# Narrow attentions: dividing and projecting each batch inside the steps, with the head sums passed through DRAM

## Time and profile before

| | us |
|---|---|
| median of 3 runs | 1738.42 (1737.92 to 1742.84) |
| profiled execution, its own time | 1742.06 |
| its span, first to last instruction | 1740.3 |
| PE busy | 1470.2 (84%) |
| DVE busy | 1009.0 (58%) |
| ACT busy | 797.1 (46%) |
| POOL busy | 455.9 (26%) |

### The profile page before, as it was taken

One profiled execution on the slowest core, in us unless ns is written; L12 is line 12 of the kernel. 1 busy time (PEld: TensorE's weight loads), 2 busy tenths in 40 slices (PEclk: granted clock), 3 DMA queues, 4 the chain that ended last, 5 costly groups with the idle time before them and its releaser, 6 DMA issues. The chain is left out here.

```text
span 1740.3 us, 30717 instructions
## 1 busy us (share of the span) xinstructions
PE 1470.2 (84%) x10727; PEld 738.2 (42%) x10747; DVE 1009.0 (58%) x1970; ACT 797.1 (46%) x1479; POOL 455.9 (26%) x658
## 2 busy tenths in 40 slices
PE   7998999999749999679876898889836888888887
PEld 5777634444424445246533442222404333433354
DVE  5665598884352222465547578997274574567335
ACT  3554537677213333215330136777434365346535
POOL 6121300000144443320126230000003354245311
PEclk9999999999969999699887898999957899989878
DMA  2000443110200000001000163121001520342000
GB/s 95 1 0 0 146 161 93 42 49 8 117 0 0 1 0 0 0 7 49 5 6 0 57 198 110 50 54 29 15 0 44 169 70 21 98 157 66 11 16 24
DMA packets 82246, 85.67 MB, mean 49 GB/s; under 512 B 7228, under 2 KB 67900, under 8 KB 81756
## 3 DMA queue, kind: packets, MB, share of 16 engines
q1 hardware_dynamic: 82152, 84.45, 15.2%
HBM read 51.33 MB, written 32.51 MB: 48 GB/s over the span
## 5 line engine op out<-in xcount | busy, mean ns | idle before, releaser
L1282 ACT ACTIVATE arena<-ps 128x1024 f32<-128x1024 f32 x256 | 261.9, 1023 | 112.1 <-PE ps L1191 111.2
L1176 PE MATMUL ps<-k_stack,q_stack 49*128 49x512 bf16 x512 | 192.3, 387 | 15.3 <-DVE small L1306 13.2
L1191 PE MATMUL ps<-q_stack,k_stack 51*128 51x256 bf16 x1024 | 191.3, 275 | 0.5 <-ACT arena L1282 0.4
L1303 DVE CUSTOM_DVE_ANT_0 small<-ps,mask_b 128x512 bf16<-128x512 f32 x256 | 168.0, 689 | 33.7 <-PE ps L1176 32.3
L1306 DVE TENSOR_REDUCE small<-ps 128x1 f32<-128x512 f32 x256 | 162.1, 685 | 22.6 <-PE ps L1176 21.6
L1492 DVE TENSOR_REDUCE small<-ps 128x6 f32<-128x768 f32 x128 | 122.6, 958 | 77.8 <-PE ps L1374 75.7
L1203 PE MATMUL ps<-arena,v_pad 128*32 128x256 f32 x2048 | 163.7, 394 | 1.1 <-ACT arena L1282 1.1
L1468 ACT ACTIVATE arena<-ps 128x384 f32<-128x384 f32 x256 | 117.8, 488 | 76.5 <-PE ps L1393 75.8
L1076 POOL TENSOR_SCALAR_AFFINE_SELECT arena<-arena 128x256 f32<-128x256 f32 x256 | 101.9, 406 | 84.2 <-ACT arena L1468 84.0
L2543 DVE TENSOR_TENSOR arena<-ps,arena 128x512 f32<-128x512 f32 x64 | 44.3, 692 | 120.8 <-PE ps L2509 120.8
L2558 POOL TENSOR_TENSOR arena<-arena 128x512 f32<-128x512 f32 x64 | 80.9, 1264 | 108.9 <-DVE arena L2543 107.1
(11 more groups left out here) (353 smaller groups left out, 3036.2 us busy)
## 6 DMA issues: line engine op xcount, KB each, us to landing
q_stack<-q_scratch SPq DMA_DIRECT2D x128, 96.0 KB
k_stack<-k_scratch SPq DMA_DIRECT2D x64, 192.0 KB
k_scratch<-arena SPq DMA_DIRECT2D x8, 768.0 KB, 3.6
k_stack<-k_scratch SPq DMA_DIRECT2D x64, 96.0 KB
q_scratch<-arena SPq DMA_DIRECT2D x4, 1152.0 KB, 5.4
arena<-in_ctxT SPq DMA_DIRECT2D x8, 512.0 KB, 6.6
k_scratch<-arena SPq DMA_DIRECT2D x8, 512.0 KB, 4.7
k_scratch<-arena SPq DMA_DIRECT2D x16, 256.0 KB, 4.5
```

What stands on the lines that cost most here:

```text
L1176: pe.matmul(ps[:, t, :], c.q_stack[par][64 * e:64 * e + ROW_MAX, pr, t * P:(t + 1) * P], c.k_stack[par][64 * e:64 * e + ROW_MAX, pr, :], s ...
L1191: mm = pe.matmul(ps[:, bank, (ch % 2) * S:(ch % 2 + 1) * S], c.k_stack[prv][64 * e:64 * e + ROWS, pr, ch * P:(ch + 1) * P], c.q_stack[prv] ...
L1282: act.activation(buf.probs[i % 8], ps[:, bank:bank + 2, :].rearrange("p a n -> p (a n)"), ACT.Exp, scale=scale).then_inc(g["probs"].sem, 1)
L1303: dve.tensor_tensor_reduce(buf.junk[t], ps[:, t, :], c.mask_b[:, M_X + t * SC:M_X + (t + 1) * SC], 1.0, FLOOR, op0=ALU.add, op1=ALU.max, a ...
```

## The change

The stage `combine` is removed. A new class `Outputs` does its work for batches 0 to 4 inside the steps, four steps behind the scores, and for batches 5 to 7 behind the last step, in the same block.

For each batch b except the last, SP stores the 128 rows of summed groups (512 KB) to a DRAM scratch in step b+2, and loads the numerators back as 128 rows of 256 columns (128 KB), and the denominators as 128 rows of 32 columns (16 KB); DVE inverts these in step b+3 (`invert`, with the guard where there is one); SP stores the inverses (16 KB) and loads them spread over the 8 channels of a head (128 KB). In step b+4 the quotient is taken (POOL in the wide attentions, DVE in the short ones), multiplied by the gate on POOL where there is one, and projected by PE at position 7 into bank 7; in the wide attentions ACT copies the result with its bias and POOL adds it to x, in the short ones DVE adds it. Before PE writes head sum group 1 into bank 7 again it waits for that copy, or that addition. Behind the last step batch 5 is finished, batch 6 is inverted as 128 rows of 256 columns, and batch 7's sums are collected, inverted and spread by PE without DRAM.

`attend_steps` writes steps 0 to 3 and 8 out and loops over 4 to 7. The gate is made in `project`, in front of its `keep_clock`. The constants are loaded in two parts. In the feed-forward of the last layer some semaphores have other names.

```diff
@@ project @@
+            if gated:
+                for t in TS:
+                    if t < 2:
+                        pe.wait_ge(g["ln_scaled"].sem, g["ln_scaled"].at(4))
+                    else:
+                        pe.wait_ge(g["gate_out"].sem, g["gate_out"].at(t - 1))
+                    pe.matmul(ps[:, 2 + t % 2, :], w[:, W_G:W_G + P], norm.tile(c.xn, t), start=True, stop=True)\
+                      .then_inc(g["gate_in"].sem, 1)
...
             keep_clock(c, pe, PARTS_WAIT, bank=bank_of(kind, n))
...
+            if gated:
+                for t in TS:
+                    act.wait_ge(g["gate_in"].sem, g["gate_in"].at(t + 1))
+                    act.activation(norm.tile(c.xn, t), ps[:, 2 + t % 2, :], ACT.Sigmoid, bias=w[:, W_BG:W_BG + 1])\
+                       .then_inc(g["gate_out"].sem, 1)
@@ Outputs @@
+    def store_sums(self, buf, sp, b):
+        for i in range(2):
+            sp.wait_ge(g[f"summed_out{i}"].sem, g[f"summed_out{i}"].at(2 * b + 2))
+        sp.dma_start(c.sum_scratch[b, :, :, :].rearrange("r j m -> j r m"), ...).then_inc(g["sums_stored"].sem, 16)
+    def load_sums(self, sp, b, last=False):
+        sp.wait_ge(g["sums_stored"].sem, g["sums_stored"].at(16 * (b + 1)))
+        if b > 1:
+            done, n = self.quotient(b - 2)
+            sp.wait_ge(done.sem, done.at(n + 1))
+        sp.dma_start(self.num[b % 2], c.sum_scratch[b, 0:DH, :, :].rearrange("d j (k n) -> (d j k) n", n=S)).then_inc(sem, 16)
+        if last:
+            self.spread(sp, self.rec[b % 2], c.sum_scratch[b, DH, :, :].rearrange("j (k n) -> (j k) n", n=S), sem)
+        else:
+            sp.dma_start(self.den[b % 2], ...).then_inc(sem, 16)
+    def store_inverse(self, sp, b):
+        sp.wait_ge(g["inverted"].sem, g["inverted"].at(b + 1))
+        sp.dma_start(c.inv_scratch[b, :, :].rearrange("q (a n) -> (q a) n", a=P // H), self.den[b % 2]).then_inc(g["inv_stored"].sem, 16)
+    def spread_inverse(self, sp, b):
+        sp.wait_ge(g["inv_stored"].sem, g["inv_stored"].at(16 * (b + 1)))
+        self.spread(sp, self.rec[b % 2], c.inv_scratch[b, :, :], g[f"inv_spread{b % 2}"].sem)
+    def finish_pe(self, buf, pe, scored):
+        self.project(pe, 1, B - 3, 0)
+        self.project(pe, 0, B - 2, 1)
+        for k in range(GROUPS):
+            den = pe.matmul(c.ps[0:H, 3, 0:S], ..., buf.summed[:, B - 1, k, :], ...)
+            num = pe.matmul(c.ps[:, 4, 0:S], ..., buf.summed[:, B - 1, k, :], ...)
+        keep_clock(c, pe, 6, bank=2)
+        pe.wait_ge(g["inverted"].sem, g["inverted"].at(B))
+        pe.matmul(c.ps[:, 5, 0:S], c.consts[0:H, C_ROWS:C_ROWS + P], self.rec[1][0:H, :], ...)
+        self.project(pe, 1, B - 1, 2)
+    def finish_dve(self, dve):
+        self.divide(dve, 1, B // 2 - 2, "last_quotient")
+        self.add(dve, B - 3, 0)
+        inverse(0, B - 2, P, self.rec[0])
+        dve.tensor_tensor(self.quot[0], self.num[0], self.rec[0], ALU.mult)
+        self.add(dve, B - 2, 1)
+        inverse(1, B - 1, H, c.ps[0:H, 3, 0:S])
+        dve.tensor_tensor(self.quot[1], c.ps[:, 5, 0:S], self.num[1], ALU.mult)
+        self.add(dve, B - 1, 2)
@@ attend_transfers @@
         if s:
             place(s - 1, 1)
+        if s > 2:
+            outs.store_inverse(sp, s - 3)
+        if s > 1:
+            outs.store_sums(buf, sp, s - 2)
         if s in (1, 2):
             store_parts(c, sp, "k", nk, s + 1, s + 2, g[f"stored_k{s + 1}"].sem)
         if 1 <= s < B - 1:
             load(s + 1, 0)
         if s < B:
             place(s, 0)
+        if s > 1:
+            outs.load_sums(sp, s - 2, s == B)
+        if s > 2:
+            outs.spread_inverse(sp, s - 3)
@@ attend_pool @@
+        if late and not causal:
+            outs.divide(pool, par, it - 2)
...
+            if late and outs.gated and i == 4:
+                outs.gate(pool, par, s - 4)
...
+        if late and not causal:
+            pool.wait_ge(g["out_kept"].sem, g["out_kept"].at(s - 3))
+            pool.tensor_tensor(xb, xb, outs.kept[par], ALU.add).then_inc(g["residual"].sem, 1)
@@ sum_waits @@
+    if grp == 1 and late:
+        pe.wait_ge(g[emptied].sem, g[emptied].at(b - 2))
@@ attend_short, PE and DVE @@
+                    if late and i == 7:
+                        project_late(c, outs, pe, s, par)
...
+                    if late and pr == 1:
+                        outs.divide(dve, par, it - 2)
+                    if (late or par) and before and pr == 2:
+                        outs.invert(dve, 1 - par, it - 2 + par, s - 3)
+                    if late and pr == 3:
+                        outs.add(dve, s - 4, 7)
@@ narrow_attention @@
-    combine(c, slot, **how)
```

More of the change, by code:

```diff
@@ L727, in store_parts, with project @@
         eng.dma_start(scratch[:, r:r + count, at], src).then_inc(sem, 16)
-def project(c, slot, name, nk, from_ctx, key_mask):
+def project(c, slot, name, nk, from_ctx, key_mask, gated):
     nc, g, ps = c.nc, c.sig, c.ps
@@ L1004, in attend_transfers @@
+def attend_transfers(c, buf, outs, sp, nk, key_mask):
     g = c.sig
@@ L1058, in attend_pool, with step @@
     pool.wait_ge(g["cleared"].sem, g["cleared"].at(1))
-    def step(it, par, front, back, before):
+    def step(it, par, front, back, before, late):
         s = it * 2 + par
@@ L1127, in attend_halves, with sum_waits @@
         pe.wait_ge(placed.sem, placed.at(s * 32))
-def sum_waits(c, pe, grp, b, first, front, ready="probs"):
+def sum_waits(c, pe, grp, b, first, front, late, ready="probs", emptied="out_kept"):
     g = c.sig
@@ L1236, in step @@
                     if back and n >= 0:
-                        sum_piece(n // 4, n % 4, b, prv, first, front)
+                        sum_piece(n // 4, n % 4, b, prv, first, front, late)
                     if before and n < 0:
@@ L1260, in keep, with step @@
                 act.wait_ge(g["summed"].sem, g["summed"].at(b * GROUPS + grp + 1))
-                act.activation(buf.summed[:, grp, bass.ds(b * S, S)], ps[:, 6 + grp % 2, 0:S], ACT.Identity)\
+                act.activation(fold(buf.summed[:, bass.ds(b, 1), grp, :].rearrange("p a n -> p (a n)"), (S,)), ps[:, 6 + grp % 2, 0:S], ACT.Identity)\
                    .then_inc(g[f"summed_out{grp % 2}"].sem, 1)
-            def step(it, par, front, back, before):
+            def step(it, par, front, back, before, late):
                 first = isinstance(it, int) and it == 0
@@ L1283, in step @@
                                        scale=scale).then_inc(g["probs"].sem, 1)
+                    if late and i == 7:
+                        act.wait_ge(g["out_proj"].sem, g["out_proj"].at(s - 3))
+                        act.activation(outs.kept[par], ps[:, 7, 0:S], ACT.Identity, bias=outs.w[:, W_BO:W_BO + 1])\
+                           .then_inc(g["out_kept"].sem, 1)
                     if before and i in (1, 5):
@@ L1394, in logits, with sum_piece @@
                       .then_inc(g["logits"].sem, 1)
-            def sum_piece(grp, piece, b, par, first, front=True):
+            def sum_piece(grp, piece, b, par, first, front=True, late=False):
                 if piece == 0:
-                    sum_waits(c, pe, grp, b, first, front, "masked")
+                    sum_waits(c, pe, grp, b, first, front, late, "masked", "residual")
                 for j in range(4):
```

314 lines of the change are left out of this document (171 added, 143 removed).

## The result

The changed kernel takes **1863.4 us** (median of four runs, 1861.1 to 1865.3) against 1738.2 for the kernel before, timed beside it (median of four, 1735.5 to 1742.8): 1.072 times, with an interval of 1.069 to 1.074. The prediction, 1736 with a range to 1749, missed it by 127 us.

The account below looks back on a forecast made before the run. The removed stage was short (74.8 us at most), PE nearly full in the masked wide steps, and the clock halves after idling. Attentions at +0.1, +0.6, -0.3, -3.0 gave -2.6 from 1738.42: 1736 us, range 1724 to 1749.

Parts of the forecast that it names:

- The price of the store: Third attention's tail: the 512 KB store of sums lands after 4.7 us, taken from its nearest measured row.
- The estimate of 3.2 us: Same store, alternative landing time: about 2.0 us plus bytes over 436 GB/s; third attention would save 4.4 us.
- 0.6 in the third tail: Third attention's end: batch 5's spread inverse, behind batch 6's store and load on SP, 0.6 us late (0 to 3).
- The slower rival: Short attentions: SP's queue becomes the bound, maxima land behind 512 KB, 1 us more per step, 12 us: 1748; chance 0.23.
- SP's cycle of 13.1 us against 13.4: Short steps: SP's placings, loads, issues and stand take 13.1 us against a lengthened step of 13.4; decides from 13.4 on.
- Wide: forecast +2.8 and +3.3: Steps of masked and unmasked wide attentions: added projections and inversions cost 2.8 us (1.0 to 5) and 3.3 (1.5 to 6).
- Short: forecast +3.0 each: Short attentions: 0.65 us a step for four steps plus 0.4; SP's queue adds 0.5 in the third, 0.8 and 0.5 gated.
- absorbed additions: Short steps: DVE's addition makes bank 7 about 1.1 us late, absorbed by PE's existing 0.83 us stand at position 11.
- The tails: Last head sum to last addition: 12.9, 12.9, 13.5, 15.3 us, 1.7 for half clock included; under 11 or over 15 is wrong.
- nine times 0.43: Tail: batch 6's projection and PE's eight collecting matmuls for batch 7, 0.43 us each, denominators ready at 7.0.
- The gate: Gated project stage: gate matmuls ahead of the holding ones, PE waiting 2.6 us; price 3.7 us (3.2 to 4.5).
- the likeliest case: Whole kernel: within 0.3% (5.2 us) of before, savings at the ends paid in the steps; chance 0.41.

Follow-up runs that it names:

- e9: The kernel before with only the change's store added, one 512 KB transfer per batch, never read or waited for: 1826.6 us, 1.049.
- e13: The kernel before with only a store of nine rows of each group (144 KB) added, in four transfers: ratio 1.000.
- e14: e9 with SP's wait for the store's landing added, where the changed kernel reads back, without the reading: ratio 1.045.
- e12: e2 with the reading back a step later in the two short attentions alone: 1758.8 us (ten runs), 1.011 against the kernel before.
- e7: e2 with the projection matmuls of the batches inside the steps one column wide instead of 256: 1748.0 us, single run.
- e16: e7 with DVE's division and addition of late batches in the short attentions also one column wide: 1752.4 us, single run.
- e1: The changed kernel with the same 512 KB store sent as four transfers of 32 partitions: 1764.3 us.
- e2: e1 with only the nine rows of each group that are read back, 144 KB instead of 512 KB: 1759.1 us.
- e5: The changed kernel with the sums read back a step later, behind the next step's first load, store still one transfer: 1910.7 us.
- e6: e2 with the sums read back a step later, behind the next step's first load: 1799.0 us.
- e3: The changed kernel with both stores (inverse, sums) issued behind the next load and the placing of maxima, still one transfer: 1957.3 us.
- e4: e2 and e3 together, 144 KB in four transfers issued behind the load and the placing: 1790.6 us.

## Why the prediction was wrong, by its own steps

**The price of the store: the step that failed.** The prediction took 4.7 us to landing from the 512 KB store of `k_scratch`. Same bytes, another shape: that one has 128 partitions outermost on both sides, this one four outermost rows in DRAM, and took 10.1. The row was chosen by size alone, and the bounds put on the price had nothing above it. The estimate of 3.2 us from the Trainium skill's section "Anatomy of one DMA" was further off: that section gives its formula for DMAs issued through GpSimd, while this store is on SP's queue, and the rate in it, 436 GB/s, is that of all sixteen engines. The other section of the Trainium skill, named above, whose rule gives four engines, was not used. The second half of the step is that the price was charged only where someone waits for the landing (0.6 in the third tail), and the store's effect on other transfers was put at nothing; e9 shows 87 us where no one waits.

**The slower rival had the place right and the mechanism half.** "The maxima land behind 512 KB" was there, at 1 us for each of 12 steps. Measured in e9: 36 us in each short attention. Its other half, SP's cycle of 13.1 us against 13.4, is not what costs these 36: e13's four issues and e14's standing cost nothing. The size was wrong twice. The wait is up to 7.4 us, not one; and behind each stand of 3 us or more for maxima in the changed kernel's short steps the work ran at half clock for at least the next 2 us (the 1.08 above); in e9 the lower clock is 13 of the 36 us. The rival had left it out though the earlier trace rows had shown it.

**The steps without the thin store.** e12, with its ten runs, stands for them. Wide: forecast +2.8 and +3.3; measured 203.6 and 182.8, +3.4 and +4.0. Right within its bounds. Short: forecast +3.0 each (1 to 6), with 0.5 and 1.3 more for SP's queue; measured 104.0 and 109.2, +5.8 and +8.8, the upper bound and beyond. The projection is at most 0.7 to 2.6 of that (e7) and DVE nothing that shows (e16), which fits the prediction's absorbed additions. The readings of 144 KB (128 and 16; e16's expectation has 176) and the spreading of 128 KB a step, to which the prediction gave a place in SP's queue but no weight in the DMA engines, are the likeliest rest; no run takes them out, so this is not shown.

**The tails.** From the last head sum to the last addition the forecast was 12.9, 12.9, 13.5 and 15.3 us. The changed kernel has 13.9, 16.6, 22.0 and 22.5, three of them over the 15 that the prediction named as a sign of being wrong; e12 has 12.4, 15.2, 14.9 and 18.5. As savings, by the ends of the table: forecast 2.7, 2.7, 3.8 and 11.0 (20.2 in all); in e12 3.2, 0.3, 1.8 and 7.7 (13.0). The two wide ones differ only by execution (15.7 to 18.6 in e1, e2 and e12). The last one is short by 3.3, and the changed kernel shows why (timeline of its end: batch 5's division, the first and last collecting matmuls, L1127 and L1131, and the last addition):

```profile
1768.18 0.42 DVE L1091 TENSOR_TENSOR arena<-arena 128x256 f32<-128x256 f32 x1 [6.15 <-DMA arena<-inv_scratch]
...
1775.72 1.04 PE L1127 MATMUL ps<-arena,consts 128*16 128x256 f32 x2
...
1776.69 1.22 PE L1131 MATMUL ps<-arena,consts 128*128 128x256 f32 x2
...
1777.84 0.61 PE L1127 MATMUL ps<-arena,consts 128*16 128x256 f32 x2
...
1780.17 0.61 PE L1127 MATMUL ps<-arena,consts 128*16 128x256 f32 x2
...
1780.71 0.70 PE L1131 MATMUL ps<-arena,consts 128*128 128x256 f32 x2
...
1785.88 0.48 DVE L1113 SCALAR_TENSOR_TENSOR xT<-ps,att_w,xT 128x256 f32<-128x256 f32 x1 [1.59 <-PE ps L1105]
```

The term was "nine times 0.43". At full clock the pair's first takes 0.54 (1780.17 to 1780.71) and its second 0.70 with its fill, at half the two take 0.97 and 1.15; the eight ran from 1775.72 to 1781.41, 5.7 us instead of 3.5. In e2, where more of them ran at half, they took 7.1. The prediction had 1.7 us for the half clock beside this term, so 2 of e2's 3.3 us lie here. The first row is the thin store again: DVE waited 6.15 us for batch 5's spread inverse, 0.86 in e2, close to the "0.6 late" when the store is short.

**The gate.** Forecast +3.7 (3.2 to 4.5) with the holding matmuls last. They are last. From ACT's last part to the attention's first instruction it was 6.5 us (1511.29 + 0.63 to 1518.45) and is 11.2 (1583.83 + 0.63 to 1595.63): +4.6, and +5.3 to the first exponential, +6.4 in e12. PE's wait for the sigmoids, forecast at 2.6, is 2.63. Behind it the third and fourth gate matmul took 3.67 (the row above), where two float32 ones of 512 columns have 1.98 at full clock: the half clock (granted 0.50 from 1587 to 1590), which the forecast had as its upper end and should have had as its value, since it had named the wait.

**The chances.** With the store spread, the sum was still wrong in sign: 1.011 instead of 0.999. So even the likeliest case was too low by some 22 us: 7 in the tails, 3 at the gate, 7 in the short steps, 1 in the wide ones, which makes 18. The profiled executions of e12 and before give the rest only roughly: the starts of the second and third attention were 3 us shorter, nearly 4 us lie outside the attentions (3 of them ahead of the first), and the kernel before ran 3.6 us above its median there.

## What to carry to other kernels

Before a transfer is priced by its bytes, write down the outermost dimension of both its sides as issued: a rearrangement that puts a 4 in front of 128 partitions makes a store that took 10.1 us instead of 2.2 for each of four spread parts, and small transfers issued behind it wait (by the Trainium skill's rule it is 128 KB on each of four engines). A store that nobody waits for is not free; ask which latency-bound transfers (here the 4 KB of maxima) are issued within its flight. And look for the price of a wait on PE in what follows it too, since behind each stand of 3 us or more for maxima the work ran at half clock here.

## What the runs showed that was not expected

Two transfers in place of one made the store slower (14.0 us against 10.1), four landed in 2.2 us each (128 KB): the count of transfers does not explain it, their outermost dimension does. Half a megabyte a step costs 87 us thin, 13 us spread, and 144 KB of it, spread, nothing. The issue of one of SP's loads stretched from 0.44 to 2.17 us behind the thin store (up to 2.46 in e9); what held it is not shown. And moving the wait for a landing out of SP's queue (e5, e6) or behind it (e3, e4) cost 30 to 94 us each time, when it was done in all four attentions, so no other place tried for these transfers was better.
